# A graph-attention and token-mixer layer on one core: edge batches reordered on four engines

## What is computed

```python
K = _type_proj(node_features, node_types, Wk, bk).reshape(n, H, DK)
Q = _type_proj(node_features, node_types, Wq, bq).reshape(n, H, DK)
V = _type_proj(node_features, node_types, Wv, bv).reshape(n, H, DK)
Ks, Qt, Vs = (K[src], Q[tgt], V[src])
for t in range(ET):
    mask = edge_types == t
    Ke = jnp.einsum('ehd,dk->ehk', Ks, Wa[t])
    Ve = jnp.einsum('ehd,dk->ehk', Vs, Wm[t])
    scores = jnp.sum(Ke * Qt, -1) * inv_sqrt_dk * relation_pri[t]
    scores = jnp.where(mask[:, None], scores, -jnp.inf)
    w = jax.nn.softmax(scores, axis=0)
    msgs = msgs + jnp.where(mask[:, None, None], w[..., None] * Ve, 0.0)
agg = jax.ops.segment_sum(msgs.reshape(-1, OUT_DIM), tgt, num_segments=n)
```

## Time and profile before

| what | value |
|---|---|
| median of 3 runs | 1062.67 us (1059.62 to 1066.2) |
| profiled execution, first to last instruction | 1151.2 us |
| edge stage in it: first to last `products` | 252.1 to 873.9 us |
| `subtract`, first to last start (48 batches apart) | 282.4 to 880.1 us |
| mean granted clock of TensorE | 0.857 |

### The profile page before, as it was taken

How to read it: one execution, slowest core, us unless ns; L and a number is a source line. 1 busy time by engine, 2 the same in 40 slices (tenths; PEclk the granted TensorE clock), 3 DMA queues, 4 the chain that set the end, 5 groups by cost and what they waited for, 6 DMA issues and landing times.

```text
span 1151.2 us, 18271 instructions
## 1 busy us (share of the span) xinstructions
PE 925.1 (80%) x5153; PEld 678.8 (59%) x5153; DVE 790.9 (69%) x1682; ACT 598.7 (52%) x1540; POOL 600.2 (52%) x745
## 2 busy tenths in 40 slices
PE   5989999933676777777778777777777978999998
PEld 4767777622444454545445555545444976788886
DVE  7756666524676885787778867877776864998541
ACT  2656766622555675667666767667654212322220
POOL 4516777672566655555666656656564044664000
PEclk9999999965777887778878878888776898999999
DMA  9725666664677776776777767767761672321020
GB/s 291 221 66 184 237 216 217 222 217 126 178 214 205 226 210 188 204 223 188 210 218 226 202 201 218 223 197 227 210 201 57 188 237 74 97 79 37 1 88 25
DMA packets 126204, 202.76 MB, mean 176 GB/s; under 512 B 19755, under 2 KB 94846, under 8 KB 126102
## 3 DMA queue, kind: packets, MB, share of 16 engines
q0 software_dynamic: 38992, 129.87, 37.4%
q1 hardware_dynamic: 76630, 61.86, 17.6%
q10 hardware_dynamic: 10480, 9.83, 2.5%
HBM read 160.50 MB, written 40.99 MB: 175 GB/s over the span
## 4 chain that ended last, share of the span: by engine, by line
PE 45%; DVE 17%; issue 14%; ACT 10%; POOL 5%; another core or an unknown queue 4%; DMA 3%; SPq 1%; DVEq 0%; ACTq 0%; POOLq 0%
PE ps L1611 7%; PE ps L1594 5%; PE ps L2423 5%; PE ps L913 4%; PE ps L2410 4%; DVE big L1824 4%; PE ps L954 2%; PE ps L2374 2%; PE ps L925 2%; PE ps L901 2%; ACT edge L1466 2%; DVE big L1765 2%; POOL big L2272 2%; PE ps L1620 2%
## 5 line engine op out<-in xcount | busy, mean ns | idle before, releaser
L1389 POOL DMA_INDIRECT big<-kv_scratch,src_i x392 | 370.9, 946 | 257.5 <-PE ps L1611 120.8
L1594 PE MATMUL ps<-edge 64*128 64x256 f32 x784 | 145.2, 501 | 35.3 <-issue 22.5
L1611 PE MATMUL ps<-big,edge 128*64 128x256 f32 x784 | 138.1, 485 | 31.0 <-issue 13.8
L1765 DVE TENSOR_TENSOR big<-big,ps 128x1024 f32<-128x1024 f32 x98 | 118.5, 1209 | 44.1 <-remote 34.5
L1594 PEld LDWEIGHTS ps<-edge 64*128 64x128 f32 x784 | 86.6, 238 | 62.1 <-issue 50.2
L1772 DVE TENSOR_REDUCE ps<-big 128x32 f32<-128x1024 f32 x98 | 119.4, 1218 | 0.1
L1488 ACT ACTIVATE edge<-ps 128x256 f32<-128x256 f32 x98 | 37.6, 383 | 153.3 <-PE ps L1611 99.7
L1824 DVE TENSOR_TENSOR big<-big,ps 128x1024 f32<-128x1024 f32 x98 | 116.6, 1208 | 0.0
L1611 PEld LDWEIGHTS ps<-big,edge 128*64 128x64 f32 x784 | 60.8, 166 | 85.3 <-issue 62.7
L1620 PE MATMUL ps<-ident,edge 128*128 128x128 f32 x196 | 49.5, 341 | 70.3 <-ACT edge L1488 60.9
L1466 ACT ACTIVATE edge<-edge 128x64 f32<-128x64 f32 x392 | 102.9, 334 | 0.0
(11 more groups left out here) (346 smaller groups left out, 1837.1 us busy)
## 6 DMA issues: line engine op xcount, KB each, us to landing
edge<-q_scratch SPq DMA_DIRECT2D x196, 64.0 KB
big<-kv_scratch,src_i POOLq DMA_INDIRECT x392
edge<-key_scratch SPq DMA_DIRECT2D x98, 64.0 KB
agg_scratch<-big SPq DMA_DIRECT2D x16, 252.0 KB
xn_scratch<-big ACTq DMA_DIRECT2D x5, 640.0 KB
mix_scratch<-big SPq DMA_DIRECT2D x25, 128.0 KB
mix_x_scratch<-big SPq DMA_DIRECT2D x25, 128.0 KB
wmix<-mix_x_scratch ACTq DMA_DIRECT2D x25, 128.0 KB
```

What stands on the lines that cost most here:

```text
L1389: pool.indirect_dma_start(kv_slots[s][:, k, :], None, kv_d[0:N, :], bass.IndirectOffsetOnAxis(ap=src_i[:, e:e + 1], axis=0)).then_inc(got[ ...
L1594: ins = pe.matmul(qr_ps[g % 2][:, (2 * hg + k) * D:(2 * hg + k + 1) * D], ohT[64 * hg:64 * hg + 64, g % 2, k * P:(k + 1) * P], qwin[64 * h ...
L1611: ins = pe.matmul(sums_of(g)[64 * hg:64 * hg + 64, :], oneh[:, s, k, hg * 64:hg * 64 + 64], kv_slots[s][:, 2 * hg + k, D:2 * D], start=(k ...
L1765: dve.tensor_tensor(k_rows, k_rows, qr_ps[g % 2].rearrange("p (k d) -> p k d", d=D), ALU.mult).then_inc(pr, 1)
```

## The change

It rewrites the order of the work of a batch on DVE, PE and ACT and gives the node sums two tiles in place of one.

- DVE: `maxima(b)` and `maximum(b)` stand in the batch's own turn, `maxima` ahead of the two older messages and `maximum` behind them. Before, both stood in the next turn, between the products. `subtract(b-1)` still stands behind the second product of the next turn; `mark` stands ahead of `weights`.
- PE: both `window_sums` of the older batch stand at the end of the turn, one ahead of and one behind `spread_maxima`. `turn_maxima` stands just before. `target_rows` of the next batch stand at the start and behind the second `turn_sums`.
- ACT: the two `keep_rows` of a batch stand early in the turn, with `distances` around them; the two `keep_sums` together behind the exponential, then both `onehots`, then `mix_gelu` of the batch's own h product. Before, the gelu stood one turn later, ahead of `keep_rows` and the exponential.
- The sums of even groups stay in bank 2; those of odd groups go to the upper half of bank 1 (`turn_ps`), where the maxima and the totals have their lower half; `ysum` has two halves. The one-hot ring shrinks from six to four (`OHRING`), which pays for that in SBUF.
- New waits: `subtract` also waits for `keep_rows` of the last odd group, the odd `turn_sums` for `subtract`, `totals` for `keep_sums` of the odd group, and the one-hots for the node sums of four groups back in place of six.

POOL's and SP's orders are the same. No instruction of arithmetic or DMA goes or comes.

```diff
@@ -32,6 +32,7 @@
...
 RING_BIG = RING
+OHRING = 4
@@ -254,12 +255,12 @@
...
         dist = edge.take(2 * P)
-        oneh = edge.take(RING, 2, P)
+        oneh = edge.take(OHRING, 2, P)
...
         mx = edge.take(2, P)
-        ysum = edge.take(D)
+        ysum = edge.take(2, D)
@@ -1310,15 +1311,16 @@
...
             sum_ps = ps[2][:, 0:2 * P]
+            turn_ps = [sum_ps, ps[1][:, 2 * P:4 * P]]
...
-                return own_ps[g] if g in own_ps else sum_ps
+                return own_ps[g] if g in own_ps else turn_ps[g % 2]
...
             def rows_of_sums(g):
-                return own_rows[g] if g in own_rows else ysum
+                return own_rows[g] if g in own_rows else ysum[:, g % 2, :]
@@ -1326,6 +1328,9 @@
...
             h_ps_e, y_ps_e = ps[0][:, 0:D], ps[0][:, D:2 * D]
+
+            def odd_kept(b):
+                return min(2 * b, NG - 4)
@@ -1465,9 +1470,9 @@
...
                     ins.then_inc(gp, 1)
-                    at_least(act, yd, g - RING + 1)
+                    at_least(act, yd, g - OHRING + 1)
                     act.wait_ge(gp, g + 1)
-                    act.activation(oneh[:, g % RING, :, :].rearrange("p k m -> p (k m)"), gap.rearrange("p a m -> p (a m)"),
+                    act.activation(oneh[:, g % OHRING, :, :].rearrange("p k m -> p (k m)"), gap.rearrange("p a m -> p (a m)"),
@@ -1513,29 +1518,24 @@
...
                 distances(0)
-                for b in range(-1, NB - 1):
-                    keep_sums(2 * b - 4)
-                    if b >= 0:
-                        distances(2 * b + 2)
+                distances(1)
+                for b in range(NB):
+                    distances(2 * b + 2)
+                    keep_rows(2 * b - 4)
...
                         load_x1(m)
-                    for m in mix_tiles(b, 1):
-                        mix_gelu(m)
...
                     keep_rows(2 * b - 3)
+                    distances(2 * b + 3)
                     exponentials(b - 1)
+                    keep_sums(2 * b - 4)
+                    keep_sums(2 * b - 3)
                     onehots(2 * b)
-                    keep_sums(2 * b - 3)
-                    distances(2 * b + 3)
-                    keep_rows(2 * b - 2)
                     onehots(2 * b + 1)
-                keep_sums(NG - 6)
-                keep_rows(NG - 5)
-                exponentials(NB - 2)
-                onehots(NG - 2)
-                keep_sums(NG - 5)
-                onehots(NG - 1)
+                    for m in mix_tiles(b, 0):
+                        mix_gelu(m)
+                keep_rows(NG - 4)
@@ -1549,7 +1549,6 @@
...
                 factors_exp(1)
-                keep_rows(NG - 4)
@@ -1604,11 +1603,11 @@
...
                     else:
-                        at_least(pe, ue, g)
+                        at_least(pe, ue, g - 1)
...
                         for hg in range(2):
-                            ins = pe.matmul(sums_of(g)[64 * hg:64 * hg + 64, :], oneh[:, s, k, hg * 64:hg * 64 + 64],
+                            ins = pe.matmul(sums_of(g)[64 * hg:64 * hg + 64, :], oneh[:, g % OHRING, k, hg * 64:hg * 64 + 64],
@@ -1616,6 +1615,8 @@
...
                     pe.wait_ge(ye, g + 1)
+                    if g % 2 and g not in own_ps:
+                        pe.wait_ge(sbt, (g + 1) // 2 + 1)
@@ -1625,6 +1626,7 @@
...
                     pe.wait_ge(exd, b + 1)
+                    at_least(pe, ue, odd_kept(b))
@@ -1674,33 +1676,24 @@
...
                 pe.wait_ge(s_ed, 1)
-                for b in range(-1, NB - 1):
+                target_rows(0)
+                target_rows(1)
+                for b in range(NB):
...
                         turn_bases(1)
-                    target_rows(2 * b + 1)
+                    target_rows(2 * b + 2)
                     turn_sums(2 * b - 4)
-                    turn_maxima(b - 1)
-                    window_sums(2 * b - 3)
-                    spread_maxima(b - 1)
-                    turn_sums(2 * b - 3)
...
                         mix_y(m)
+                    turn_sums(2 * b - 3)
+                    target_rows(2 * b + 3)
                     totals(b - 1)
-                    target_rows(2 * b + 2)
-                    window_sums(2 * b - 2)
...
                         mix_h(m)
-                target_rows(NG - 1)
-                turn_sums(NG - 6)
-                turn_maxima(NB - 2)
-                window_sums(NG - 5)
-                spread_maxima(NB - 2)
-                turn_sums(NG - 5)
-                totals(NB - 2)
-                turn_maxima(NB - 1)
-                spread_maxima(NB - 1)
-                window_sums(NG - 4)
-                window_sums(NG - 3)
+                    turn_maxima(b)
+                    window_sums(2 * b - 2)
+                    spread_maxima(b)
+                    window_sums(2 * b - 1)
@@ -1804,6 +1797,7 @@
...
                     dve.wait_ge(mB, b + 1)
+                    at_least(dve, ye, odd_kept(b))
@@ -1924,40 +1918,27 @@
...
                 float_bases(c)
-                for b in range(NB - 1):
+                for b in range(NB):
                     products(2 * b)
-                    maxima(b - 1)
                     head_sums(2 * b)
-                    maximum(b - 1)
...
                     head_sums(2 * b + 1)
-                    weights(b - 1)
-                    mark(b)
...
                         mix_row(m)
-                    messages(2 * b - 2)
+                    mark(b)
+                    weights(b - 1)
...
                         mix_stats(m)
+                    maxima(b)
+                    messages(2 * b - 2)
                     messages(2 * b - 1)
+                    maximum(b)
...
                         search(c, b - SEARCH_AT, 1)
-                products(NG - 2)
-                maxima(NB - 2)
-                head_sums(NG - 2)
-                maximum(NB - 2)
-                products(NG - 1)
-                subtract(NB - 2)
-                head_sums(NG - 1)
-                weights(NB - 2)
-                mark(NB - 1)
-                maxima(NB - 1)
-                messages(NG - 4)
-                maximum(NB - 1)
-                messages(NG - 3)
```

## The result

The changed kernel takes 1035.39 us (median of 4 runs, 1032.45 to 1036.41), the kernel before 1064.43 (4 runs, 1059.62 to 1069.39). The ratio is 0.972, with a 95% interval of 0.968 to 0.976: 29 us faster, inside the range of 985 to 1066 and near the forecast of 1028.

A forecast was written before the change was run, and what follows sets the result against it. A ring of waits between ACT and PE, no full engine, bounds the edge stage. 12.45 to 11.2 us a batch gives 60 us of profile, 55 timed; 35 taken between 9 and 55 gives 1028, range 985 to 1066.

The forecast's parts named there:

- A: Changed edge stage: PE's in-order chain is the new pace, at partly better rates, 1028 us; chance 0.48.
- ends of 9 and 90 us: Gain in timed runs: 9 us if late semaphores exist under the profiler alone, 90 us if PE reaches full speed.
- PE's sum: PE's work and unhidden waits after the change, 9.6 to 13.2 us by kind of batch, mean 11.2 against 12.45.
- A ring is cut.: Two sum tiles let node sums follow one another; one-hots (1.65 us), distances and gelu (1.91) leave the ACT-PE ring.
- The batch before, 12.45 us: Edge stage before: `subtract` runs once a batch, 282.4 to 880.1, so 597.7 / 48 = 12.45 us.
- fast bound of the prediction: PE's 9.4 us a batch falls by an eighth if less idling brings full speed; gain 97 us of profile.
- Rival B: Edge stage: PE speeds up, POOL's gathers at 9.6 us and DVE pace nearly all; 90 us gain, 973; chance 0.18.
- Rival C: The ring seen in the timeline is largely lateness of the profiled execution; gain 9 us, 1054; chance 0.20.
- Rival D: PE's new order stalls in series, 13.3 us a batch; 38 us slower, 1100; decides above 3.05 us idle; chance 0.14.
- The table load.: ACT in batches with gelu: a load costs 1.28 us without drain, not the 2.66 of the skill's page.
- DVE: the subtraction behind the next two products is cover.: DVE: two products and a head sum, some 3.6 us, cover a 3.9 us path; 0.3 us at worst shows.
- The signs to look for.: `subtract` every 11.2 to 11.8 us; node-sum waits ACT under 50, POOL under 60; PE waits about 1 us, above 80% busy.

The follow-up runs named there:

- gather test: Three gathers in place of four for each group behind the first six: on the kernel before 1056.93 us (0.993), on the changed kernel 1008.92 us (0.946).
- second profile: The kernel before, unchanged, profiled once more: time 1069.3 us, span 1067.6.

## Why the prediction was right, point by point

- **The forecast, 1028, faster by 35 us.** 29 were measured. The sign, the place and, as far as the runs test it, the mechanism of the gain held: no engine but a ring of waits paced the stage, and the second tile is needed to cut it. What paces the changed kernel came out otherwise than in A, as the points below say. The size was a choice between ends of 9 and 90 us, and the two batch times under it were both too long, by 1.5 and 0.9 us: that 35 came near 29 is in good part luck. With the batch before put right alone, at 10.94, PE's sum of 11.2 after would have said slower.
- **"A ring is cut."** Shown in the main: one tile for the kept rows costs 41 us in the new order, and the gather test shows that POOL's work was not the pace before (8 us for a quarter of it). Not shown is what the tiles give without the new order. And of the ring's parts the gelu with its 1.9 us, which the prediction named, bears nothing: moved back it costs 0, and on the kernel before a later gelu costs 65 us.
- **The batch before, 12.45 us.** This was the mis-sized term. It was 10.94 in an ordinary execution. The prediction saw the sign of it (the span 88.5 us longer than the median, 52 us of late semaphores) and gave it as one bound, 11.4, for which it took the 52 us alone; with all 88.5 us laid on the 48 batches it would have had 10.6, and the measured 10.94 lies between. Of the 1.5 us too much, 1.0 was PE's busy time, 9.4 us for 8.4, at the lower clock. The lateness was not a cost of the profiler: the second profiled execution has no remote wait ahead of the subtraction. Nor was PE always fuller than shown, which the estimated ends of the Trainium skill's page "Perfetto Trace Analysis" (Tensor Engine Instruction) would allow: in the second profile the modelled ends and the waits behind them agree (node sums from 562.92 for 1.08 us, the waiting kept rows at 564.06).
- **PE's sum, 11.2 us a batch after.** It failed, with its sequence of waits. PE's work is 391.2 / 47.4 = 8.25 us a batch, the fast bound of the prediction, and its idle time 98.4 / 47.4 = 2.1 us. The batch is 10.33. The change did not bring that faster work: in the second profile of before PE's work is 8.4 already. The error of 0.9 here and that of 1.5 in the batch before went the same way, so that their difference, 1.25 less half by judgment, came out near 0.61.
- **Rival B, POOL's issue as the floor.** Its mechanism is what happened after the change: 10.0 of 10.33 us, three gathers give 26 us, half the bytes a third of that. Its batch of 10.4 us, its DMA share of 84% (0.82) and its sign held too: no batch with mixer products takes over 12 us (the longest 11.94). Its price, 90 us, was wrong because it was counted from 12.45. The floor of 9.6 us was 0.4 too low: it was averaged over gathers whose issue was hidden in a wait.
- **Rival C, nothing to measure.** Its reason (the seen ring was largely lateness) was half true, its price not: 29 us were left.
- **Rival D, PE's new waits.** The waits exist, but are small: 23.4 us in all for the subtraction, 0.5 a batch against the 0.9 feared, and 11 us is what the move that takes this wait and ACT's away is worth. Idle time stayed under the 3.05 us from which it decides.
- **The table load.** Right: the exponential's load starts at 527.71, takes 1.28 us, and the function follows at 529.00.
- **"DVE: the subtraction behind the next two products is cover."** Right on the order before, wrong on the new one, where it costs 11 us.
- **The signs to look for.** ACT's wait for node sums fell to 44 us and POOL's to 24, and the subtraction waits 2.4 us in all. PE above 80% and 1 us a batch of waiting for messages came out as 0.80 and 0.5. The main sign failed: the subtraction runs every 10.33 us, not every 11.2 to 11.8.

What stays open: why that one execution of the kernel before was 8% longer, which was seen once, and the kernel's timed runs don't show it; and how much of the slower variants' price is the lower clock.

## What to carry to other kernels

Hold a profile's span against the timed runs before its waits are priced. Where it is 8% longer, profile again: scaling the batch to the runs would have left it at 12.45 x 0.923 = 11.5 us here, where a second profile showed 10.94. When two groups share one tile between engines, count the ring of hand-overs first: without its second SBUF tile the new order is slower than the old one. And price a move in the order it is made in: the same one-line move of the subtraction cost 41 us with the old order and gained 11 with the new. After a ring is cut, look for cover that has turned into delay.

## What was not expected of the hardware

- One execution of the same program had PE's semaphores up to 2.4 us late, remote waits of 31.0 us ahead of the subtraction, a mean granted clock of 0.79 in the stage and a span of 1151.2 us; the next profiled one had none of these, 0.88 and 1067.6.
- Halving the bytes of the gathers (DMA share 0.82 to 0.53) moved the time by 8 us, cutting their number by a quarter by 26: a gather of 128 rows takes POOL 0.95 us and 0.3 of issue whether its rows have 1 or 2 KB.
- In the profiled executions a longer batch mostly goes with a lower granted clock in the stage: 0.91 at 10.14 us (the maximum between the messages), 0.88 at 10.94 (the kernel before, second profile), 0.83 at 11.38 (the maxima in their own turn), and 0.78 to 0.80 at the three from 12.01 to 12.45. Which of the two leads is not shown.
